# A chunked state-space scan beside a feed-forward net: carried state for two heads at once, and projections gathered into the down product

## The reference, cut to what matters

```python
# state-space part, 4 heads of 64, state of 128
def step(h, inp):
    dA_t, dtx_t, B_t, C_t = inp
    h = h * dA_t[:, :, None, None] + dtx_t[..., None] * B_t[:, :, None, :]
    y_t = jnp.einsum('bhpn,bhn->bhp', h, C_t)
    return (h, y_t)
...
y = jnp.swapaxes(ys, 0, 1) + D[None, None, :, None] * xh
y = y.reshape(batch, L, D_INNER) * jax.nn.silu(z)
return residual + jnp.einsum('bli,di->bld', y, out_proj_w)

# feed-forward part, 128 -> 512 -> 512 -> 512 -> 128
h = jax.nn.silu(_tlin(x, w1_w, w1_s)) * _tlin(x, w2_w, w2_s)
h = jax.nn.gelu(_tlin(h, h1_w, h1_s), approximate=False)
h = jax.nn.gelu(_tlin(h, h2_w, h2_s), approximate=False)
return _tlin(h, w3_w, w3_s)
```

## Time and profile before

| what | value |
|---|---|
| runs, us | 630.19, 630.77, 632.46; median 630.77 |
| profiled execution, us | 632.69, its span 630.92 |
| TensorE matmul busy (PE) | 582.4 us, 92% |
| ScalarE busy (ACT) | 453.5 us, 72% |
| VectorE busy (DVE) | 371.0 us, 59% |
| GpSimd busy (POOL) | 142.8 us, 23% |
| granted TensorE clock, mean | 0.984 |

### The profile page before, as it was taken

How to read it: one execution, slowest core, us unless ns; L and a number is a source line. 1 busy time by engine, 2 the same in 40 slices (tenths; PEclk the granted TensorE clock), 3 DMA queues, 4 the chain that set the end, 5 groups by cost and what they waited for, 6 DMA issues and landing times.

```text
span 630.9 us, 11320 instructions
## 1 busy us (share of the span) xinstructions
PE 582.4 (92%) x4048; PEld 345.5 (55%) x4053; DVE 371.0 (59%) x1022; ACT 453.5 (72%) x602; POOL 142.8 (23%) x171
## 2 busy tenths in 40 slices
PE   4669999999999999999897899799989999999998
PEld 4324334444343333333334477478767888888887
DVE  7884765646444353475516765683276676676753
ACT  2368988999989999989666275555766576566663
POOL 2043222020110011002700745103003131222231
PEclk9878999999999999999989999999999999999999
DMA  7112002013422220210317220200000000000000
GB/s 229 29 34 68 2 1 68 1 41 105 169 96 92 101 85 1 69 68 9 109 26 224 67 73 39 80 2 0 0 1 1 2 18 0 1 18 1 2 17 18
DMA packets 31175, 31.00 MB, mean 49 GB/s; under 512 B 6912, under 2 KB 21024, under 8 KB 31120
## 3 DMA queue, kind: packets, MB, share of 16 engines
q1 hardware_dynamic: 29872, 27.71, 14.0%
q0 software_dynamic: 1248, 2.57, 1.1%
HBM read 13.44 MB, written 12.89 MB: 42 GB/s over the span
## 4 chain that ended last, share of the span: by engine, by line
PE 64%; DVE 19%; ACT 7%; issue 5%; POOL 2%; SPq 1%; DMA 1%; DVEq 0%; POOLq 0%; ACTq 0%
PE ps L1311 18%; PE ps L1292 9%; PE ps L92 4%; PE ps L94 4%; PE ps L93 4%; PE ps L1622 2%; PE ps L1388 2%; PE ps L1375 2%; DVE r L2449 1%; PE ps L1488 1%; PE ps L1204 1%; DVE r L2388 1%; ACT r L958 1%; DVE r L2385 1%; SPq L706 1%
## 5 line engine op out<-in xcount | busy, mean ns | idle before, releaser
L958 ACT ACTIVATE r<-ps 128x1024 f32<-128x1024 f32 x272 | 258.4, 1034 | 34.2 <-PE ps L1292 31.7
L1311 PE MATMUL ps<-r 128*32 128x512 f32 (+3 forms) x1280 | 147.9, 549 | 2.2 <-DVE r L2043 1.0
L835 POOL TENSOR_SCALAR_AFFINE_SELECT r<-r 128x512 f32<-128x512 f32 (+1 forms) x80 | 47.8, 602 | 218.7 <-ACT r L958 218.4
L1292 PE MATMUL ps<-r2r 32*128 32x512 f32 (+3 forms) x640 | 79.3, 452 | 8.1 <-DMA r2r<-r2r 4.3
L1292 PEld LDWEIGHTS ps<-r2r 32*128 32x128 f32 x640 | 34.8, 186 | 51.4 <-ACT r L958 20.8
L873 POOL TENSOR_TENSOR r<-r 128x512 f32<-128x512 f32 x16 | 23.1, 1446 | 139.0 <-ACT r L1129 139.0
L1311 PEld LDWEIGHTS ps<-r 128*32 128x32 f32 x1280 | 28.0, 109 | 42.7 <-issue 30.3
L94 PE MATMUL ps<-r2r 128*128 128x512 f32 x112 | 44.3, 395 | 0.0
L93 PE MATMUL ps<-r2r 128*128 128x512 f32 (+1 forms) x96 | 35.8, 372 | 0.0
L813 POOL DMA_INDIRECT rows_by_expert<-r x16 | 17.8, 1110 | 63.2 <-DVE r L1958 59.4
L1129 ACT ACTIVATE r<-r 128x512 f32<-128x512 f32 x16 | 10.1, 633 | 28.7 <-DVE r L2449 28.7
(11 more groups left out here) (405 smaller groups left out, 1208.5 us busy)
## 6 DMA issues: line engine op xcount, KB each, us to landing
rows_by_expert<-r SPq DMA_DIRECT2D x34, 258.0 KB, 2.5
r2r<-r2r SPq DMA_DIRECT2D x60, 64.0 KB, 2.0
r<-in_f_W SPq DMA_DIRECT2D x1, 2048.0 KB, 9.3
r<-rows_by_expert SPq DMA_DIRECT2D x23, 64.5 KB, 1.8
res<-in_x SPq DMA_DIRECT2D x4, 256.0 KB, 4.1
r<-in_g_h1T SPq DMA_DIRECT2D x1, 1024.0 KB, 5.7
r<-in_g_h2T SPq DMA_DIRECT2D x1, 1024.0 KB, 7.9
r<-rows_by_token SPq DMA_DIRECT2D x4, 256.0 KB, 3.9
```

The lines of the kernel that those rows point to most:

```text
L835: pool.affine_select(blk, blk, pattern, ALU.is_ge, nothing, base=0, channel_multiplier=-1).then_inc(s_msk, 1)
L958: act.activation(probs[:, n % PBUFS, :, :], ps[:, b:b + 2, :], ACT.Exp).then_inc(s_exp, 1)
L1292: m = pe.matmul(ps[:, 2 * (n % SBUFS) + h, at:at + TB - query], kst[32 * j:32 * j + 32, group, P * kt:P * kt + P], qst[32 * j:32 * j + 32, ...
L1311: m = pe.matmul(ps[32 * j:32 * j + 32, 6, query:TB], vp[:, kt, group, :], probs[:, (2 * v + j // 2) % PBUFS, j % 2, at:at + TB - query], s ...
```

## The change

The carried state is multiplied with the chunk's C as it is, for two heads in one matmul (their 2 x 64 columns side by side), into bank 3; there is no `cs` any more. The decay since the chunk's start, `ec`, depends on the token, and is multiplied in afterwards by VectorE (`carried`), which then adds the result to `yg`. So `ec` is needed only for the head that a partition belongs to: two exponentials on 64 partitions each instead of one over four heads, and a third, of four columns, for the decay over the whole chunk (`elast`). GpSimd's second product is gone. The projections of chunks 0, 1 and 2 of each block (and of chunk 15) are added up in the block's down product behind its matmuls; that of chunk 3 of blocks 0, 1 and 2 stays a step of its own, into bank 0, with an addition by VectorE once a block. `yg` is kept for four chunks.

```diff
-        xnTh, xnTl = xnr[:, :], r2r[:, 12292:14340]
+        xnTh, xnTl = xnr[:, :], r2r[:, 12288:14336]
...
@@ gpsimd
                 pool.tensor_tensor(mm[:, b], ed[:, b], along(gm[:, b, :], NH), ALU.mult).then_inc(s_cm, 1)
-                pool.wait_ge(s_ce, 2 * i + 2)
-                if not i:
-                    pool.sem_inc(s_cm, 1)
-                    continue
-                pool.tensor_tensor(cs[:, b], ec[:, b], along(CT[:, P * i:P * i + P], NH), ALU.mult
-                                   ).then_inc(s_cm, 1)
@@ scalar, decays
-                    act.wait_ge(s_cm, 2 * (i - 1))
                     act.wait_ge(s_ch, i)
-                act.activation(ec[:, b], ps[:, 1, :].rearrange("p (h t) -> p h t", h=NH), ACT.Exp).then_inc(s_ce, 1)
+                sums_ = ps[:, 1, :].rearrange("p (m r t) -> p m r t", m=MI, r=2)
+                if i:
+                    for r in range(2):
+                        rows_ = slice(PD * r, PD * r + PD)
+                        m = act.activation(ec[rows_, b], sums_[rows_, :, r, :], ACT.Exp)
+                if i < NCH - 1:
+                    m = act.activation(elast[:, b], sums_[:, :, :, P - 1].rearrange("p m r -> p (m r)"), ACT.Exp)
+                m.then_inc(s_ce, 1)
@@ tensor, down
-                    joined = TPB * b + i == NCH - 1
-                    dst = ps[:, 3, 0:D] if joined else ps[:, ffn_bank("DOWN", b, 0), P * i:P * i + P]
-                    if joined:
-                        pe.wait_ge(s_ca, NCH - 1)
+                    own = i < TPB - 1 or b == NB - 1
+                    final = TPB * b + i == NCH - 1
+                    dst = ps[:, 0, 0:D] if final else ps[:, ffn_bank("DOWN", b, 0), P * i:P * i + P]
                     for k in range(FO):
                         m = pe.matmul(dst, fc[k][:, P * i:P * i + P], f3[:, k, :], start=(k == 0),
-                                      stop=(k == FO - 1 and not joined))
+                                      stop=(k == FO - 1 and not own))
+                    if own:
+                        pe.wait_ge(s_cg, TPB * b + i + 1)
+                        for m_ in range(MI):
+                            m = pe.matmul(dst, yg[:, i, m_, :], owT[:, m_, :], start=False, stop=(m_ == MI - 1))
@@ tensor, chunk
+                if i > TPB:
+                    pe.wait_ge(s_ca, (i - 1) // TPB)
@@ tensor, state
-                pe.wait_ge(s_cm, 2 * i + 2)
+                pe.wait_ge(s_ch, i + 1)
+                if i:
+                    for m_ in range(MI):
+                        pe.matmul(ps[:, 3, P + P * m_:2 * P + P * m_],
+                                  hst[:, 2 * m_:2 * m_ + 2, :].rearrange("p h d -> p (h d)"),
+                                  CT[:, P * i:P * i + P], start=True, stop=True)
+                pe.wait_ge(s_cm, i + 1)
                 pe.wait_ge(s_cx, 2 * i + 2)
-                pe.wait_ge(s_ch, i + 1)
                 for h in range(NH):
-                    m = pe.matmul(dst, dtx[:, b, h, :], mm[:, b, h, :], start=True, stop=(i == 0))
-                    if i:
-                        m = pe.matmul(dst, hst[:, h, :], cs[:, b, h, :], start=False, stop=True)
+                    m = pe.matmul(dst, dtx[:, b, h, :], mm[:, b, h, :], start=True, stop=True)
@@ vector, state_carried
-                    step.mark(dve.tensor_tensor(hst, hst, over(ec[:, b, :, P - 1], PD), ALU.mult))
+                    step.mark(dve.tensor_tensor(hst, hst, over(elast[:, b, :], PD), ALU.mult))
...
-                if i >= 2:
-                    dve.wait_ge(s_co, i - 1)
+                if i:
+                    step.mark(dve.tensor_tensor(carried, ps[:, 3, P:P + DI].rearrange("p (m t) -> p m t", m=MI),
+                                                ec[:, b], ALU.mult))
+                n = i % TPB
+                if i >= TPB:
+                    dve.wait_ge(s_f4, i // TPB)
+                    if n == TPB - 1:
+                        dve.wait_ge(s_co, i // TPB)
...
+                if i:
+                    step.alone(dve.tensor_tensor(yg[:, n], yg[:, n], carried, ALU.add))
+                dve.tensor_tensor(yg[:, n], yg[:, n], z2[:, :, P * i:P * i + P], ALU.mult).then_inc(s_cg, 1)
@@ vector, slots
                     if s % 2:
-                        if s >= 3:
-                            chunk_added(s // 2 - 1)
                         if o == 1 and b:
+                            last_chunk_added(b - 1)
                             finished(b - 1)
```

More of the change, by code:

```diff
@@ L329, in build @@
         ed = r3[:, c0 + 256:c0 + 1280].rearrange("p (b h t) -> p b h t", b=2, h=NH)
-        ec = r3[:, c0 + 1280:c0 + 2304].rearrange("p (b h t) -> p b h t", b=2, h=NH)
+        ec = r3[:, c0 + 1280:c0 + 1792].rearrange("p (b m t) -> p b m t", b=2, m=MI)
+        elast = r3[:, c0 + 1792:c0 + 1800].rearrange("p (b h) -> p b h", b=2)
         mm = r3[:, c0 + 2304:c0 + 3328].rearrange("p (b h t) -> p b h t", b=2, h=NH)
-        cs = r3[:, c0 + 3328:c0 + 4352].rearrange("p (b h t) -> p b h t", b=2, h=NH)
+        yg = r3[:, c0 + 3328:c0 + 4352].rearrange("p (n m t) -> p n m t", n=TPB, m=MI)
         dtx = r3[:, c0 + 4352:c0 + 4864].rearrange("p (b h d) -> p b h d", b=2, h=NH)
@@ L335, in build @@
         hst = r3[:, c0 + 5376:c0 + 5632].rearrange("p (h d) -> p h d", h=NH)
-        yg = r3[:, c0 + 5632:c0 + 6144].rearrange("p (b m t) -> p b m t", b=2, m=MI)
+        carried = r3[:, c0 + 5632:c0 + 5888].rearrange("p (m t) -> p m t", m=MI)
         ps = ctx.enter_context(nc.psum_tensor("ps", [P, 8, 512], F32))
@@ L1658, in state, with projected @@
                               start=True, stop=True).then_inc(s_cst, 1)
[L1660 to L1663, removed]
+            def projected(b):
+                pe.wait_ge(s_cg, TPB * b + TPB)
                 for m_ in range(MI):
-                    m = pe.matmul(ps[:, 3, 0:D], yg[:, i % 2, m_, :], owT[:, m_, :],
+                    m = pe.matmul(ps[:, 0, P + DI:P + DI + D], yg[:, TPB - 1, m_, :], owT[:, m_, :],
                                   start=(m_ == 0), stop=(m_ == MI - 1))
@@ L1673, in chunk_units @@
                         chunk(s // 2 + 1)
-                elif s:
-                    projected(s // 2 - 1)
+                elif s and s // 2 % TPB == 0:
+                    projected(s // 2 // TPB - 1)
             pe.wait_ge(s_cvr, 2 * NB)
@@ L2445, in chunk_started @@
                 if i >= 2:
-                    dve.wait_ge(s_cm, 2 * (i - 1))
+                    dve.wait_ge(s_cm, i - 1)
                     dve.wait_ge(s_cst, i - 1)
@@ L2468, in state_carried @@
                     dve.wait_ge(s_ce, 2 * i + 2)
-                    step.mark(dve.tensor_tensor(hst, hst, over(ec[:, b, :, P - 1], PD), ALU.mult))
+                    step.mark(dve.tensor_tensor(hst, hst, over(elast[:, b, :], PD), ALU.mult))
                 else:
                     dve.wait_ge(s_cy, NCH)
-                if i >= 2:
-                    dve.wait_ge(s_co, i - 1)
+                    dve.wait_ge(s_ce, 2 * i + 2)
+                if i:
[6 more added lines that the diff above has]
+                        dve.wait_ge(s_co, i // TPB)
                 for m_ in range(MI):
-                    step.mark(dve.scalar_tensor_tensor(yg[:, b, m_, :], xc[:, m_, P * i:P * i + P], d2[:, m_:m_ + 1],
+                    step.mark(dve.scalar_tensor_tensor(yg[:, n, m_, :], xc[:, m_, P * i:P * i + P], d2[:, m_:m_ + 1],
                                                        ps[:, 2, P * m_:P * m_ + P], ALU.mult, ALU.add))
@@ L2480, in state_carried, with last_chunk_added @@
                                       ).then_inc(s_ch, 1)
[L2481 to L2485, removed]
+                if i:
+                    step.alone(dve.tensor_tensor(yg[:, n], yg[:, n], carried, ALU.add))
+                dve.tensor_tensor(yg[:, n], yg[:, n], z2[:, :, P * i:P * i + P], ALU.mult).then_inc(s_cg, 1)
+            def last_chunk_added(b):
+                i = TPB * b + TPB - 1
+                dve.wait_ge(s_co, b + 1)
+                dve.tensor_tensor(res[:, i, :], res[:, i, :], ps[:, 0, P + DI:P + DI + D], ALU.add).then_inc(s_ca, 1)
             def down_added(b):
                 dve.wait_ge(s_f4, b + 1)
-                dve.wait_ge(s_ca, TPB * b + TPB - 1)
                 n = TPB if b < NB - 1 else TPB - 1
@@ L2496, in finished @@
             def finished(b):
-                dve.wait_ge(s_ca, TPB * (b + 1))
+                dve.wait_ge(s_ca, b + 1)
                 dve.sem_inc(s_fin, 1)
@@ L2534, in _ @@
             dve.wait_ge(s_f4, NB + 1)
-            dve.tensor_tensor(res[:, NT - 1, :], res[:, NT - 1, :], ps[:, 3, 0:D],
+            dve.tensor_tensor(res[:, NT - 1, :], res[:, NT - 1, :], ps[:, 0, 0:D],
                               ALU.add).then_inc(s_fin, 1)
```

4 lines of the change are left out of this document (removed).

## The result

The changed kernel takes **645.59 us** (median of six runs, 644.51 to 648.01) against 631.91 for the kernel before in the runs beside it (630.19 to 633.63): 1.0225 times, 95% interval 1.0198 to 1.0252. So it is slower, as forecast, by 13.7 us where 10.0 were forecast, and 0.6 us above the end of the range. (Of the 4.8 us between 640.8 and 645.59, 1.1 us is the kernel before itself: 630.77 in the three runs shown, 631.91 in these.) Its profiled execution is the 648.01 one, with a span of 646.3 us; the one of before had 632.69 and 630.92.

The account below looks back on a forecast made before the run. TensorE was taken as the bound, with a ScalarE and VectorE path 0.80 us behind it. Lags of 2.24, 3.42, 3.42 and 0.9 us in blocks 0 to 3 gave +10.0 us: 640.8 us, range 636.0 to 645.0.

Parts of the forecast that it names:

- 0.80 us of slack: Last stage: the ScalarE and VectorE path to the block's last gelu ends 0.80 us before it would delay down.
- VectorE's term: Carried product and add inside state_carried, ahead of chunk_started in slots 2, 4 and 6: 0.79 us a slot, bounds 0.68 and 0.90.
- TensorE's state step: Full-width carried matmuls in place of half the 64-column ones: 0 us a chunk, bounds -0.2 to +0.1.
- A (hidden): Rival: VectorE's added work fits into its idle times, 632.0 us, no measurable difference; chance 0.11.
- B (TensorE cheaper): Rival: strict matmul order saves 3.3 us and the 2.1 us of waits go, 625.4 us; chance 0.05.
- The moved projections: Three a block move behind the last gelu into down, which grows by 1.34 us; TensorE comes to it 1.34 us earlier.
- ScalarE. ... So +0.17 us: Exponentials of a slot: two of 256 elements and one of four columns replace one of 512, +0.17 us, bounds 0 and 0.39.
- TensorE idle some 3 us: Sign in each of blocks 0 to 2: TensorE idle some 3 us, first about 2.4 us ahead of up(b+1, 1).
- This takes the 2.1 us of waits away: State step: without GpSimd's product with C, TensorE's 2.1 us of waits for GpSimd go, if nothing else moves.
- Rival C: Path hit at 1.3 us a slot or more, by 64-partition exponentials or strided PSUM reads, 644 to 647 us; chance 0.07.

Follow-up runs that it names:

- e1: Changed kernel with chunk_started ahead of state_carried in slots 2, 4 and 6: 624.79 us, 0.9925 of the kernel before.
- e6: Changed kernel with one exponential of 256 columns on 128 partitions in place of the two on 64: 638.61 us, 1.0103 of the kernel before.
- e9: Changed kernel without the projections of chunks 0, 1 and 2 of each block in down: 641.76 us, 1.0131 of the kernel before.
- e10: Changed kernel with its two exponentials both starting at partition 0, one on 128 partitions and one on 64: 642.5 us, 1.0124 of the kernel before.
- e7: Kernel before with two unread VectorE instructions of 128x256 ahead of chunk_started in slots 2, 4 and 6: 636.57 us, ratio 1.0125.
- e8: Kernel before with two unread VectorE instructions of 128x256 behind weighted in slots 2, 4 and 6: 633.03 us, ratio 1.0013.
- e5: Changed kernel with ten overwritten matmuls of 512 columns ahead of last(b, 1) in blocks 0 to 2: 643.36 us, 1.0167 of the kernel before.
- e3: Kernel before with only the projections moved into down, cs and GpSimd's second product kept: 630.37 us, ratio 1.005.
- e12: Kernel before with two unread VectorE instructions of 128x256 ahead of chunk_started in one slot a block: 635.05 us, ratio 1.0019.
- e13: Changed kernel run again, unchanged: 647.58 us, 1.0199 of the kernel before.
- e4: Kernel before with chunk_started ahead of state_carried in slots 2, 4 and 6: 636.84 us, ratio 1.0148.

## Why the prediction was right in its mechanism and short by 3.4 us

**Right.** The bound behind TensorE was named: the path over ScalarE and VectorE that ends with the last gelu, with 0.80 us of slack. e1, e6, e9 and e10 each bear out a term of it; e7 against e8 bears out that the place on VectorE decides. VectorE's term came out at its 0.79, and TensorE's state step cost 0.05 us more and not less. Of the rivals, A (hidden) falls with the idle 2.6 us ahead of up(b+1, 1); B (TensorE cheaper) with the state step of 1.13 us. The moved projections did cost 1.34 us a block, because down's inputs didn't come earlier (e9).

**Wrong, the term "ScalarE. ... So +0.17 us".** It measured 0.36. The distance of 0.28 us came from two short exponentials of an earlier stage; the new pair starts at partitions 0 and 64 and stands 0.37 apart, and the four-column one behind it doesn't overlap either. In e10, with no start at 64, both overlaps are back. The sum has this term ten times, three in each of blocks 0 to 2 and one in block 3: 10 x 0.19 = 1.9 us. The value was inside the bounds that the step gave (0 and 0.39), near its upper end. The Trainium skill, VectorE: DVE Perf Modes, section on the TRN2 errata, gave about 0.29 us as an estimate; the sum by it would have been about 1 us larger, and it was the nearer one. By the same figures one instruction of 512, 256 or 4 elements takes, as an estimate, 0.57, 0.36 or 0.15 us; the traces have 0.58, 0.37 and 0.17. How far neighbours overlap isn't in them, and the overlap is what this term was about.

**Missing, the term "TensorE idle some 3 us".** The prediction said that the idle time would come, at the right place and of nearly the right length, and gave it no consequence but its own length. In block 2 the granted clock fell in it and in block 0 1.1 us behind it, at 1.46 us together (e5). 10.0 + 1.9 + 1.5 = 13.4, and 13.4 is what the stage measured, with the small errors that cancel (3.21 and 4.91 above).

**Right for a weaker reason.** "This takes the 2.1 us of waits away" is borne out. But that these waits were the mark of a second path without slack wasn't seen, and where GpSimd's second product stays, the same sum fails (e3: +1.11 instead of 0.54; e7: +2.51 instead of 1.93; e12: +0.75 instead of about 0).

**Rival C** (only the size is off, 644 to 647) is what happened, for one of its two named causes, at 1.15 us a slot and not 1.3, with the clock for the rest. It had a chance of 0.07, too little beside a term whose bounds were 0 and 0.39 and whose chosen value came from instructions of another partition range.

**Open:** why the clock fell in blocks 0 and 2 and not in block 1, whose wait (2.62 us) is as long as block 2's. Length alone doesn't decide: e10 has a fall at a wait of 2.11 us in block 2 and none at the same wait in block 1, and e9 has one in all of blocks 0 to 2. e13 repeats the changed kernel's two. The carried part alone, with the projections left in place, wasn't run.

## What to carry to other kernels

Ask of an added instruction what stands behind it on its engine: the same two cost 2.5 us a block ahead of the subtractions that ScalarE waits for and 0.5 behind, and work that loses its deadline (here through the projections' move into down) can then be put last, which made the changed kernel 0.75% faster than the one before. Before trusting a slack, look for a second path that ends in the same engine: small waits that come in every slot are its mark. When a forecast opens a new gap of 2 to 3 us in TensorE's dense work, give it a price beyond its length, or a filler.

## What the runs showed of the hardware

- **ScalarE instructions that start at partitions 0 and 64 in turn didn't overlap.** Two 64x256 exponentials from PSUM at partitions 0 and 64 are 0.37 us apart, their full duration, a 128x256 and a 64x256 one that both start at 0 only 0.27 (e10). Other pairs of partitions weren't run.
- **With one wait of 2.1 to 3.1 us in dense work TensorE's granted clock fell to 1.2 GHz** for some 3.4 us, in two of three blocks and again in a second execution, within the wait or up to 1.4 us behind it. Matmuls that filled 2.3 us of the gap kept it at 1.00 (e5), and at waits of 1.6 to 2.0 us it didn't fall (e6). A fall within the wait cost 1.2 us, one about 1 us behind it 0.3 to 0.4.
- **Two heads' 64-column matmuls run side by side, and halving their count saved nothing:** 1.08 us before, 1.13 after.
- **VectorE's instructions with all inputs in SBUF are drawn out beside GpSimd's products:** the same 128x256 instruction takes 1.51 us beside one (e8, ending 0.3 us behind it) and 0.42 without (e7). Those that read PSUM keep their 0.60 and 0.42 us beside GpSimd (e4, L2475 and L2479).
